# Accumulating transfers for three blocks of a context job's softmax sums in a two-layer gated attention and expert kernel

## The chip, the core and the metric

The kernel runs on one core of a Trainium2 chip. The metric is the device time of one execution in microseconds (us), as the median of several runs. A profile of one execution is used to read where the time goes.

## The reference

Two layers are applied to x (2 x 1024 tokens of 512 features). Each adds an attention and then a mixture of eight experts, both gated by a tanh, to the residual. The first layer's attention is causal self-attention plus attention to a context (2 x 2048 tokens of 256 features); the second's is attention to the context alone. There are 16 heads of 32 features. What matters here is the attention:

```python
att = jnp.einsum('bhqd,bhkd->bhqk', q, k) * scale
...
y = jnp.einsum('bhqk,bhkd->bhqd', jax.nn.softmax(att, axis=-1), v)
...
attc = jnp.einsum('bhqd,bhkd->bhqk', qc, kc) * scale
y = y + jnp.einsum('bhqk,bhkd->bhqd', jax.nn.softmax(attc, axis=-1), vc)
```

All of it is in float32. A softmax needs, for every query, the sum of its exponentials over all keys; the changed part is how this sum is formed.

## The kernel before

The program is a row of phases: two projections, attention with self and context jobs ("attn0"), output and routing, experts, then a projection, attention with context jobs alone ("attn1"), output and routing, experts. Only the attention phases are touched.

An attention phase works on units: one batch entry and four heads (GH = 4) of one kind, causal or context. attn0 has eight units of each kind in turn, attn1 eight context units. A unit has four query blocks of 256 queries, and each is a *job*. A context job goes over all 2048 keys, 16 blocks of 128; a causal job over the blocks up to the diagonal, 2, 4, 6 or 8 of them. A job works in steps of two blocks (STEP = 2), so a context job has eight steps, called s0 to s7 below, and a block kb belongs to step kb // 2.

In a step, each engine has its part, in an order that the loops of the phase write out:

- TensorE ("PE") makes the scores of four items, each one block and two heads (`scores`, L714), works ahead on the maxima of later jobs (`maxima`, L686), and forms the products of the step before with the values (`values`, L731).
- ScalarE ("ACT") turns each item's scores into exponentials in `probs` (`exponent`, L803). `probs` is a ring of three steps, so an exponential of step m must wait until step m - 3 has been read by TensorE (`valued`) and by GpSimd (`added`). At a job's end ACT also copies the result out of PSUM (`drain`, L812).
- VectorE ("DVE") reduces the maxima (L844) and inverts the sums (`invert`, L861), in four pieces after the job's end.
- GpSimd ("POOL") adds the blocks named in `pooled` into `psums` (L662 for the first two, L665 for the others), and six steps after a job's end multiplies its result by the inverse (`normalize`, L642).
- SyncE ("SP") loads the keys, queries and values of later units and stores results.

The sum over the keys is shared out. TensorE could form it alone, by a matmul of a block's exponentials with ones (L738), four per block, one for each head. To spare it that, GpSimd adds ten blocks of a context job (0, 1, 2, 3, 4, 6, 7, 8, 10 and 12), and TensorE multiplies the sum `psums` by ones once, at the job's end (L746), after the values of the last step, when `added` says that the last add is done. The blocks 5, 9, 11, 13, 14 and 15 go through ones one by one. All these matmuls add up in half of one PSUM bank, and the value products in the other half.

`both`, `inv` and `y` are the buffers of a job's result on its way out: DEEP = 5 of each. The drain of a job must wait until the job that had the buffer before is normalised.

## Time and profile before

| what | value |
|---|---|
| median of 3 runs | 4098.98 us (4093.19 to 4100.37) |
| profiled execution | 4095.09 us |
| its span, first to last instruction | 4093.4 us |
| granted clock of TensorE, mean | 0.947 |
| TensorE, matmuls | busy 3706.0 us (91%) |
| VectorE | busy 2546.0 us (62%) |
| ScalarE | busy 2030.1 us (50%) |
| GpSimd | busy 1742.5 us (43%) |

The profile gives, for each instruction, its line, its start and its duration; idle time of an engine is put down to what ended it. Matmuls are pipelined, so their durations overlap, and time between the starts of two pieces says more than their busy time. A float32 matmul of this kernel appears as two records, so that a block of ones, four matmuls, is "x8". The timelines merge like instructions that follow each other into one row; the view by stretches gives the busy time of each engine between two times.

### The profile page before, as it was taken

The numbers are of one execution on the slowest core, as the hardware profiler recorded it, in microseconds if no ns is written. First come the engines' busy times: TensorE is split into PE (matmuls) and PEld (weight loads), VectorE is DVE, ScalarE is ACT, GpSimd is POOL, SyncE is SP. The second block draws the span as 40 slices with busy tenths as digits, with TensorE's granted clock in tenths as the row PEclk, the third lists the DMA queues.
The fourth block names the chain that finished last, engine by engine and source line by source line (L and its number), as shares of the span: only waits on it lengthen the run. The fifth ranks groups of instructions, "written<-read, shape, count | busy, mean of one in ns | idle before, by whom it ended". The sixth has DMA issues, their size and how long they took to land. (4 is left out here: it accounts for less than half of the span.)

```text
span 4093.4 us, 77661 instructions
## 1 busy us (share of the span) xinstructions
PE 3706.0 (91%) x30860; PEld 2602.1 (64%) x30860; DVE 2546.0 (62%) x3221; ACT 2030.1 (50%) x3561; POOL 1742.5 (43%) x854
## 2 busy tenths in 40 slices
PE   6989699999999997659996699999998659999997
PEld 5768456666666664459985355555554448888886
DVE  4345787878887883666664777777773664333442
ACT  2222266666666664136662366666664134434442
POOL 0000287778767775001110588888885001111110
PEclk9999799999999999779998799999998769999999
DMA  4478724433443433346653522323302233333341
GB/s 160 168 243 290 202 59 111 104 94 83 103 107 80 102 66 113 113 158 212 212 173 122 144 77 77 78 78 79 79 27 94 90 127 115 115 115 115 107 126 22
DMA packets 290273, 485.23 MB, mean 119 GB/s; under 512 B 23104, under 2 KB 121408, under 8 KB 287936
## 3 DMA queue, kind: packets, MB, share of 16 engines
q1 hardware_dynamic: 274368, 443.01, 36.2%
q0 software_dynamic: 14080, 37.76, 3.9%
q8 instruction: 208, 3.41, 0.4%
q14 instruction: 81, 0.66, 0.1%
q10 hardware_dynamic: 1536, 0.40, 0.0%
HBM read 350.67 MB, written 130.02 MB: 117 GB/s over the span
## 5 line engine op out<-in xcount | busy, mean ns | idle before, releaser
L803 ACT ACTIVATE attn_probs<-attn_low 128x512 f32<-128x512 f32 (+1 forms) x2368 | 1234.8, 595 | 465.9 <-PE attn_low L714 349.2
L844 DVE TENSOR_REDUCE attn_parts<-attn_mx 128x4 f32<-128x2048 f32 x538 | 1232.8, 2291 | 365.1 <-PE attn_mx L686 361.6
L665 POOL TENSOR_TENSOR attn_psums<-attn_psums,attn_probs 128x1024 f32<-128x1024 f32 x536 | 1275.0, 2379 | 67.6 <-ACT attn_probs L803 2.5
L714 PE MATMUL attn_low<-attn_queries,attn_keys 97*128 97x256 f32 (+1 forms) x4736 | 915.1, 311 | 11.7 <-DMA attn_queries<-attn_topT 5.6
L714 PEld LDWEIGHTS attn_low<-attn_queries,attn_keys 97*128 97x128 f32 x4736 | 658.4, 190 | 369.7 <-ACT attn_probs L803 188.0
L731 PE MATMUL attn_low<-attn_probs,attn_values 128*32 128x256 f32 x9472 | 629.4, 383 | 1.4 <-ACT attn_probs L803 1.4
L1488 DVE TENSOR_TENSOR ffn_wL<-ffn_raw,ffn_wH 128x2048 fp32r<-128x2048 f32 x128 | 293.4, 2292 | 223.1 <-ACT ffn_wH L1443 223.1
L1443 ACT ACTIVATE ffn_wH<-ffn_raw 128x2048 fp32r<-128x2048 f32 x128 | 245.3, 1916 | 338.2 <-DMA ffn_raw<-in_L_ffn_W_dram 177.4
L662 POOL TENSOR_TENSOR attn_psums<-attn_probs 128x1024 f32<-128x1024 f32 x88 | 209.8, 2384 | 369.3 <-ACT attn_probs L803 369.3
L731 PEld LDWEIGHTS attn_low<-attn_probs,attn_values 128*32 128x32 f32 x9472 | 247.6, 109 | 182.8 <-issue 2.0
L1400 PE MATMUL ffn_up<-ffn_xH,ffn_wH 128*128 128x256 f32 (+1 forms) x1024 | 348.2, 340 | 2.7 <-DVE ffn_xL L1494 2.7
L1400 PE MATMUL ffn_up<-ffn_xH,ffn_wL 128*128 128x256 f32 (+1 forms) x1024 | 349.0, 341 | 0.0
L1400 PE MATMUL ffn_up<-ffn_xL,ffn_wH 128*128 128x256 f32 (+1 forms) x1024 | 347.9, 340 | 0.0
L686 PE MATMUL attn_mx<-attn_keysn,attn_queriesn 32*128 32x512 f32 (+3 forms) x2388 | 298.8, 493 | 51.3 <-DMA attn_queriesn<-l_queries 26.5
L1415 PE MATMUL ffn_down<-ffn_wH,ffn_hH 128*128 128x512 f32 x768 | 306.7, 399 | 0.0
L1369 POOL DMA_INDIRECT out_dram<-ffn_yo,ffn_idx_out x32 | 53.8, 1680 | 592.9 <-DVE ffn_yo L1523 463.3
L1415 PE MATMUL ffn_down<-ffn_wH,ffn_hL 128*128 128x512 f32 x768 | 304.4, 396 | 0.0
L1415 PE MATMUL ffn_down<-ffn_wL,ffn_hH 128*128 128x512 f32 x768 | 304.3, 396 | 0.0
L738 PE MATMUL attn_low<-attn_probs,keep_onesf 128*32 128x256 f32 (+1 forms) x3776 | 266.5, 373 | 0.0
L1512 DVE TENSOR_TENSOR ffn_hL<-ffn_hf,ffn_hH 128x256 fp32r<-128x256 f32 (+1 forms) x256 | 138.3, 556 | 203.3 <-ACT ffn_hH L1464 203.3
L861 DVE RECIPROCAL attn_inv<-attn_both 128x64 f32<-128x64 f32 x384 | 201.0, 536 | 70.9 <-ACT attn_both L812 70.9
L1464 ACT ACTIVATE ffn_hf<-ffn_up,ffn_b1T 128x256 f32<-128x256 f32 (+1 forms) x256 | 149.4, 584 | 160.3 <-PE ffn_up L1400 160.1
(196 smaller groups left out, 4426.5 us busy)
## 6 DMA issues: line engine op xcount, KB each, us to landing
ffn_raw<-in_L_ffn_W_dram SPq DMA_DIRECT2D x128, 1024.0 KB, 5.4
attn_keys<-l_cross_keys SPq DMA_DIRECT2D x96, 512.0 KB, 6.9
attn_queries<-l_queries SPq DMA_DIRECT2D x48, 512.0 KB, 4.8
l_cross_keys<-projc_high SPq DMA_DIRECT2D x64, 256.0 KB, 2.2
l_cross_keys<-projc_lowp SPq DMA_DIRECT2D x64, 256.0 KB, 2.5
l_cross_values<-projc_vout SPq DMA_DIRECT2D x64, 256.0 KB, 2.6
attn_keysn<-l_cross_keys SPq DMA_DIRECT2D x16, 1024.0 KB, 5.0
attn_values<-l_cross_values SPq DMA_DIRECT2D x32, 512.0 KB, 7.9
```

The costliest lines, as they stand in the source:

```text
L662: pool.tensor_tensor(ps, probs[:, m % RING, 0, :, :], at, ALU.add).then_inc(added, 1)
L665: pool.tensor_tensor(ps, ps, at, ALU.add).then_inc(added, 1)
L686: mm = pe.matmul(room[:, h, at:at + cols], QN[b][rows_h, q0:q0 + P], KN[b][rows_h, part * BLK:part * BLK + cols], start=True, stop=True)
L714: mm = pe.matmul(out[:, n0:], KS[b][0:3 * HD + 1, h, kb * P:(kb + 1) * P], QS[b][0:3 * HD + 1, h, job.qb * QB + n0:(job.qb + 1) * QB], sta ...
L731: mm = pe.matmul(acc[h * HD:(h + 1) * HD, 0, n0:], VS[b][:, kb, h * HD:(h + 1) * HD], probs[:, m % RING, i, h, n0:], start=kb == 0, stop=k ...
L738: mm = pe.matmul(acc[h * HD:(h + 1) * HD, 1, n0:], c["onesf"][:, 0:HD], probs[:, m % RING, i, h, n0:], start=False, stop=False, skip_group ...
L803: act.activation(probs[:, m % RING, i // 2, heads, n0:], sc[:, item % SC, :].rearrange("p (h q) -> p h q", q=QB)[:, :, n0:], ACT.Exp, scal ...
L844: op = dve.tensor_reduce(into, seen, AX.X, ALU.max)
L1400: mm = pe.matmul(up[ft % UP][:, 0:k], w[:, cols], x[:, ch, :], start=n == 0, stop=n == 3 * C - 1)
L1415: mm = pe.matmul(down[st][:, :], h[:, ft, st * P:(st + 1) * P], w[:, cols], start=ft == 0 and n == 0, stop=ft == FT - 1 and n == 2)
L1443: act.activation(wH[:, m % RING, :], raw[:, m % RING, :], ACT.Copy).then_inc(high_made, 1)
L1488: dve.tensor_tensor(wL[:, m % RING, :], raw[:, m % RING, :], wH[:, m % RING, :].bitcast(F32), ALU.subtract).then_inc(low_made, 1)
```

## The change

In a context job, blocks 5, 9 and 11 are no longer summed by TensorE but added to block 1 by transfers that accumulate into SBUF. The exponentials of block 1 go not into the ring but into a buffer of their own, `heap` (two of them, for jobs in turn), from which the value products of block 1 read too. GpSimd issues the three transfers, at steps s2, s4 and s5, each ahead of that step's adds. The first waits until the value products of s0 have read the heap, the second and the third until the transfer before has landed (`heap_in`). At the job's end TensorE multiplies the heap by ones, after a wait for all three. ACT, before it writes over a step of the ring, waits for the transfer that reads from it.

GpSimd's own list becomes 2, 3, 4, 6, 7, 8, 10, 12 and 13: nine blocks and eight adds, where there were ten and nine. Blocks 0, 14 and 15 go through ones on TensorE. Causal jobs have no heap and keep their lists. DEEP becomes 3.

```diff
--- before.py
+++ after.py
@@ -421,7 +421,8 @@
         if unit.causal:
             self.pooled = [kb for kb in whole if kb < 2 or kb % 2 == 0]
         else:
-            self.pooled = [kb for kb in whole[:-3] if kb < 4 or kb == 7 or kb % 2 == 0]
+            self.pooled = [2, 3, 4, 6, 7, 8, 10, 12, 13]
+        self.heaped = () if unit.causal else (1, 5, 9, 11)
 
     def adds(self, step=None):
 
@@ -517,6 +518,19 @@
         done = sum(x.adds() for x in self.jobs if x.last < m)
         return done + sum(x.adds(m - x.first) for x in self.jobs if x.first < m <= x.last)
 
+    def heaps(self, j):
+
+        return sum(max(0, len(x.heaped) - 1) for x in self.jobs[j % 2:j:2])
+
+    def heaped_at(self, m):
+
+        if not 0 <= m < self.steps:
+            return 0, 0
+        job = self.jobs[self.job_of[m]]
+        s = m - job.first
+        return (len([kb for kb in job.heaped[1:] if kb // STEP == s]),
+                len([kb for kb in job.heaped[1:] if kb // STEP <= s]))
+
     def ends(self, m):
 
         j = self.job_of[m]
@@ -531,7 +545,7 @@
     plan = Plan(units)
     jobs, N_STEPS, N_JOBS = plan.jobs, plan.steps, len(plan.jobs)
     KEYS = max(u.keys for u in units)
-    RING, SC, DEEP = 3, 3, 5
+    RING, SC, DEEP = 3, 3, 3
     ROWS = GH * QB // P
     with Phase(nc, name) as ph:
         KS = [ph.sb(f"keys{b}", [P, GH, KEYS], F32R) for b in range(BUFS)]
@@ -548,6 +562,7 @@
         inv = [ph.sb(f"inv{d}", [P, QB]) for d in range(DEEP)]
         y = [ph.sb(f"y{d}", [P, QB]) for d in range(DEEP)]
         fence = ph.sb("fence", [P, BLK])
+        heap = [ph.sb(f"heap{d}", [P, GH, QB]) for d in range(2)]
         low = ph.ps("low", (P, SC + 1, BLK))
         mx = ph.ps("mx", (P, GH, BLK))
         sc, acc = low[:, 0:SC, :], low[:, SC, :].rearrange("p (a q) -> p a q", q=QB)
@@ -565,9 +580,17 @@
         stack_in = [ph.sem(f"stack_in{b}") for b in range(BUFS)]
         row_set = [ph.sem(f"row_set{d}") for d in range(ROWS_DEEP)]
         fence_set = ph.sem("fence_set")
+        heap_in = [c["keep"].sem(f"{name}_heap_in{d}") for d in range(2)]
         inverted = [ph.sem(f"inverted{d}") for d in range(DEEP)]
         y_out = [ph.sem(f"y_out{d}") for d in range(DEEP)]
         FLAT, STACK, ROW, PIECES = 2, 11, QB // P, 4
+
+        def block_of(m, i):
+
+            j = plan.job_of[m]
+            if jobs[j].heaped and (m - jobs[j].first) * STEP + i == jobs[j].heaped[0]:
+                return heap[j % 2]
+            return probs[:, m % RING, i, :, :]
 
         def load_flat(sp, u, piece):
             unit, b = units[u], u % BUFS
@@ -651,6 +674,16 @@
                     here = [kb for kb in job.pooled if kb // STEP == s]
                     k = plan.adds(m)
                     ps = psums[:, j % 2, :, :]
+                    for n, kb in enumerate(job.heaped[1:]):
+                        if kb // STEP != s:
+                            continue
+                        pool.wait_ge(exped, plan.item[m, 2 * (kb % STEP) + 1] + 1)
+                        if n:
+                            pool.wait_ge(heap_in[j % 2], DMA * (plan.heaps(j) + n))
+                        else:
+                            pool.wait_ge(valued, job.first + job.heaped[0] // STEP + 1)
+                        pool.dma_start(heap[j % 2][:, :, :], probs[:, m % RING, kb % STEP, :, :], accum_op=ALU.add
+                                       ).then_inc(heap_in[j % 2], DMA)
                     for kb in here:
                         at = probs[:, m % RING, kb % STEP, :, :]
                         if kb == job.pooled[0]:
@@ -729,10 +762,10 @@
                     for i, (kb, n0, _) in enumerate(here):
                         for h in range(GH):
                             mm = pe.matmul(acc[h * HD:(h + 1) * HD, 0, n0:], VS[b][:, kb, h * HD:(h + 1) * HD],
-                                           probs[:, m % RING, i, h, n0:], start=kb == 0,
+                                           block_of(m, i)[:, h, n0:], start=kb == 0,
                                            stop=kb == len(job.blocks) - 1, skip_group_check=True)
                     for i, (kb, n0, _) in enumerate(here):
-                        if kb in job.pooled:
+                        if kb in job.pooled or kb in job.heaped:
                             continue
                         for h in range(GH):
                             mm = pe.matmul(acc[h * HD:(h + 1) * HD, 1, n0:], c["onesf"][:, 0:HD],
@@ -741,6 +774,11 @@
                     mm.then_inc(valued, 1)
                     if m == job.last:
                         if job.pooled:
+                            if job.heaped:
+                                pe.wait_ge(heap_in[j % 2], DMA * (plan.heaps(j) + len(job.heaped) - 1))
+                                for h in range(GH):
+                                    pe.matmul(acc[h * HD:(h + 1) * HD, 1, :], c["onesf"][:, 0:HD], heap[j % 2][:, h, :],
+                                              start=False, stop=False, skip_group_check=True)
                             pe.wait_ge(added, plan.adds(m + 1))
                             for h in range(GH):
                                 mm = pe.matmul(acc[h * HD:(h + 1) * HD, 1, :], c["onesf"][:, 0:HD],
@@ -798,9 +836,15 @@
                         act.wait_ge(valued, m - RING + 1)
                         if plan.adds(m - RING + 1):
                             act.wait_ge(added, plan.adds(m - RING + 1))
+                        new, all_of = plan.heaped_at(m - RING)
+                        if new:
+                            before = plan.job_of[m - RING]
+                            act.wait_ge(heap_in[before % 2], DMA * (plan.heaps(before) + all_of))
                     act.wait_ge(scored, item + 1)
                     heads = slice(2 * (i % 2), 2 * (i % 2) + 2)
-                    act.activation(probs[:, m % RING, i // 2, heads, n0:],
+                    if job.heaped and m == job.first and i == 2 * job.heaped[0] and plan.job_of[m] >= 2:
+                        act.wait_ge(job_done, plan.job_of[m] - 1)
+                    act.activation(block_of(m, i // 2)[:, heads, n0:],
                                    sc[:, item % SC, :].rearrange("p (h q) -> p h q", q=QB)[:, :, n0:],
                                    ACT.Exp, scale=SCALE).then_inc(exped, 1)
```

The order of the instructions shows it on GpSimd, in the second attention stage, for one context job and the first add of the next. `psums` is GpSimd's sum, `y` the result that is normalised. Before:

```order
L662 TENSOR_TENSOR attn_psums<-attn_probs 128x1024
L665 TENSOR_TENSOR attn_psums<-attn_psums,attn_probs 128x1024 x6
L642 TENSOR_TENSOR attn_y<-attn_both,attn_inv 128x256
L665 TENSOR_TENSOR attn_psums<-attn_psums,attn_probs 128x1024 x2
L662 TENSOR_TENSOR attn_psums<-attn_probs 128x1024
```

And with the change (its lines are numbered anew):

```order
L695 TENSOR_TENSOR attn_psums<-attn_probs 128x1024
L685 DMA attn_heap<-attn_probs 128x1024
L698 TENSOR_TENSOR attn_psums<-attn_psums,attn_probs 128x1024 x3
L685 DMA attn_heap<-attn_probs 128x1024
L698 TENSOR_TENSOR attn_psums<-attn_psums,attn_probs 128x1024
L665 TENSOR_TENSOR attn_y<-attn_both,attn_inv 128x256
L685 DMA attn_heap<-attn_probs 128x1024
L698 TENSOR_TENSOR attn_psums<-attn_psums,attn_probs 128x1024 x3
L695 TENSOR_TENSOR attn_psums<-attn_probs 128x1024
```

One of the six adds ahead of the normalisation, and with it the two behind, are now parted by three transfers; there are eight adds in place of nine, and three of them, not two, stand behind the normalisation.

On TensorE, from the end of one context job (s7) through s0 of the next. `low` is the PSUM tile, in one part of which scores stand and in another the results; `onesf` are the ones. Before:

```order
L738 MATMUL attn_low<-attn_probs,keep_onesf 32x256 x8
L746 MATMUL attn_low<-attn_psums,keep_onesf 32x256 x4
L714 MATMUL attn_low<-attn_queries,attn_keys 128x256 x6
L686 MATMUL attn_mx<-attn_keysn,attn_queriesn 128x512 x4
L714 MATMUL attn_low<-attn_queries,attn_keys 128x256 x2
L731 MATMUL attn_low<-attn_probs,attn_values 32x256 x8
L714 MATMUL attn_low<-attn_queries,attn_keys 128x256 x6
```

And with the change:

```order
L771 MATMUL attn_low<-attn_probs,keep_onesf 32x256 x8
L780 MATMUL attn_low<-attn_heap,keep_onesf 32x256 x4
L784 MATMUL attn_low<-attn_psums,keep_onesf 32x256 x4
L747 MATMUL attn_low<-attn_queries,attn_keys 128x256 x6
L719 MATMUL attn_mx<-attn_keysn,attn_queriesn 128x512 x4
L747 MATMUL attn_low<-attn_queries,attn_keys 128x256 x2
L764 MATMUL attn_low<-attn_probs,attn_values 32x256 x4
L764 MATMUL attn_low<-attn_heap,attn_values 32x256 x4
L771 MATMUL attn_low<-attn_probs,keep_onesf 32x256 x4
L747 MATMUL attn_low<-attn_queries,attn_keys 128x256 x6
```

The heap's matmuls stand ahead of those of psums, and s0 now has a block of ones, that of block 0.

## Rows read from the trace of the kernel before

**Rows 1.** Page of the kernel before: its span

```profile
span 4093.4 us, 77661 instructions
```

**Rows 2.** Stretch table: length, PE, PEld, DVE, ACT, POOL busy, PEclk, DMA, GB/s

```profile
2390.00:2440.00 50.00, 49.71 (x552) 29.70 (x556) 39.03 (x26) 34.24 (x68) 42.72 (x20) 1.00 0.25 60
```

**Rows 3.** Timeline of PE (start, us, operation, records), context jobs of both stages

```profile
541.97 0.61 PE L746 MATMUL attn_low<-attn_psums,keep_onesf 128*32 128x256 f32 x8
...
567.74 0.61 PE L746 MATMUL attn_low<-attn_psums,keep_onesf 128*32 128x256 f32 x8
...
2617.13 1.07 PE L731 MATMUL attn_low<-attn_probs,attn_values 128*32 128x256 f32 x16
...
2620.03 1.07 PE L731 MATMUL attn_low<-attn_probs,attn_values 128*32 128x256 f32 x16
...
2622.93 1.07 PE L731 MATMUL attn_low<-attn_probs,attn_values 128*32 128x256 f32 x16
...
2626.15 1.07 PE L731 MATMUL attn_low<-attn_probs,attn_values 128*32 128x256 f32 x16
...
2639.73 1.05 PE L738 MATMUL attn_low<-attn_probs,keep_onesf 128*32 128x256 f32 x16
2640.59 0.61 PE L746 MATMUL attn_low<-attn_psums,keep_onesf 128*32 128x256 f32 x8
...
2642.90 1.07 PE L731 MATMUL attn_low<-attn_probs,attn_values 128*32 128x256 f32 x16
```

**Rows 4.** Timeline of POOL, the same job

```profile
2616.66 2.38 POOL L662 TENSOR_TENSOR attn_psums<-attn_probs 128x1024 f32<-128x1024 f32 x1 [2.73 <-ACT attn_probs L803]
2619.18 14.99 POOL L665 TENSOR_TENSOR attn_psums<-attn_psums,attn_probs 128x1024 f32<-128x1024 f32 x6
2634.14 0.73 POOL L642 TENSOR_TENSOR attn_y<-attn_both,attn_inv 128x256 f32<-128x256 f32 x1
2634.83 4.91 POOL L665 TENSOR_TENSOR attn_psums<-attn_psums,attn_probs 128x1024 f32<-128x1024 f32 x2
```

**Rows 5.** Timeline of ACT, the same job

```profile
2621.58 2.06 ACT L803 ACTIVATE attn_probs<-attn_low 128x512 f32<-128x512 f32 x4 [0.83 <-PE attn_low L714]
...
2635.67 1.57 ACT L803 ACTIVATE attn_probs<-attn_low 128x512 f32<-128x512 f32 x3 [0.82 <-ACT attn_probs L803]
```

**Rows 6.** Instructions of L665 (the adds): who waited for them, us, times

```profile
  PE attn_low L746: 1.8, 2
```

**Rows 7.** Transfers that POOL issues: issue times, landing times, GB/s in 40 slices

```profile
L234 POOL DMA_DIRECT2D projc_xin<-in_ctx_dram x7 | 5.2, 749 | 138.5 <-DVEq L348 138.5
...
1776.00 1.00 POOL L1358 DMA_INDIRECT ffn_xg<-xn,ffn_idx  x1 [0.30 <-issue]
...
L1369 POOL DMA_INDIRECT out_dram<-ffn_yo,ffn_idx_out x32: 1549/1618/2078, 3426.7 to 4082.2; - x32
...
projc_xin<-in_ctx_dram POOLq DMA_DIRECT2D x8, 512.0 KB, 5.1
...
GB/s 0 0 0 0 0 23 0 47 79 167 82 0 0 0 0 20 79 164 123 0 0 0 0 20 61 155 138 0 0 0 0 29 76 164 105 0 0 0 0 0
...
out_dram<-ffn_yo,ffn_idx_out POOLq DMA_INDIRECT x4, 4.7
```

**Rows 8.** Stretch table and timeline of PE after a wait, columns as in rows 2 and 3

```profile
113.80:117.20 3.40, 3.40 (x11) 2.74 (x10) 1.39 (x2) 0.62 (x2) 0.00 (x0) 0.57 0.17 60
...
112.53 1.57 PE L244 MATMUL proj_turn<-keep_ident,proj_xn 128*128 128x128 f32 x8 [3.24 <-DVE proj_xL L345]
...
115.18 0.63 PE L264 MATMUL proj_bank<-proj_xH,proj_wH 128*128 128x512 f32 x1
115.61 0.63 PE L264 MATMUL proj_bank<-proj_xL,proj_wH 128*128 128x512 f32 x1
...
117.29 0.39 PE L264 MATMUL proj_bank<-proj_xH,proj_wH 128*128 128x512 f32 x1
117.52 0.39 PE L264 MATMUL proj_bank<-proj_xL,proj_wH 128*128 128x512 f32 x1
```

## The prediction

> **What bounds the kernel now.** I read the page first for the span: 4093.4 us, in a profiled execution of 4095.09 us [rows 1]. The median of the three runs shown is 4098.98 us, 3.9 us above that execution; the sum below is made against 4095.1 and then lifted by 4 us.
>
> The change touches only context jobs of the two attention stages: 8 units x 4 query blocks in each, so **64 jobs** of 8 steps (s0 to s7). The stretch table is next: in 50 us of the second attention stage TensorE is busy 49.71 us at granted clock 1.00 and GpSimd 42.72 us, with the DMA engines at a quarter [rows 2]. So TensorE sets the pace and GpSimd has some 15% to spare; the reader should ask where in a job that spare time lies.
>
> TensorE's timeline answers for one job [rows 3]. The value products (L731) of s0 begin at 2617.13 and those of the next job's s0 at 2642.90: a period of **25.77 us**. The first stage has the same period: its matmuls on psums (L746) start at 541.97 and 567.74, 25.77 apart. A step without a matmul against the ones, s1, lasts 2622.93 - 2620.03 = 2.90; s2, with one such block (four matmuls, which the trace shows as 8 records), lasts 2626.15 - 2622.93 = 3.22. One block of ones is therefore worth **0.32 us** inside a job. In s7 blocks follow each other: two start at 2639.73 and the psums at 2640.59, so **0.43 us** each there.
>
> GpSimd's timeline of the same job [rows 4]: first add at 2616.66, six at 2619.18, the normalisation of the job before at 2634.14 (0.73 us), two more adds that end at 2634.83 + 4.91 = 2639.74. That is 23.08 us, or (23.08 - 0.73) / 9 = **2.48 us per add**, without a hole. TensorE reads the psums at 2640.59, 0.85 us later, and only 2 times was seen waiting for an add there, 1.8 us in all [rows 6]. GpSimd's slack thus lies before its first add, where it waits 2.7 us for the first exponentials of the new job; against the end of the job it has 0.85 us.
>
> **The change, part by part.** I measure from the time of the first add of before (2616.66 = 0). There, the psums are read at 23.93.
>
> TensorE: blocks 5, 9, 11 and 13 lose their ones matmuls in s2, s4, s5 and s6 (4 x 0.32 = 1.28 saved); block 0 gets one in s0 (0.32 more); the heap adds one block in s7 (0.43 more). The saving is 1.28 - 0.32 - 0.43 = **0.53 us per job**; all of it falls ahead of the psums, which TensorE would want at 23.93 - 0.53 = **23.4**, with a period of 25.24. Value matmuls keep their number.
>
> GpSimd: one add of nine goes. But the first add is now of blocks 2 and 3, a step later, and the order is: add, transfer of 5, three adds, transfer of 9, add, normalisation, transfer of 11, three adds. Transfer 5 stands ahead of the add of block 4 and waits for the last exponential of s2. ACT's group at 2621.58 holds four exponentials in 2.06 us, the first of them that one [rows 5]: 2621.58 + 0.52 - 2616.66 = 5.4, and 0.3 later for the ones of block 0, so 5.8. The first add, after s1's exponentials, is over by then. From there GpSimd has 7 adds (17.4), the normalisation (0.7), three issues of d each, and a stall s: 5.8 + 17.4 + 0.7 = 23.9 + 3d + s. TensorE, which wants the psums at 23.4, is late by **L = 0.5 + 3d + s**.
>
> The stall: transfer 11 may only go when 9 has landed, X after its issue began. Between the two GpSimd has its issue d, one add (2.5) and the normalisation (0.7), so s = X - d - 3.2. Queued behind it are the adds of 10, 12 and 13, and behind those TensorE's psums, the drain on ACT and the next job. Transfer 5 has three adds (7.5 us) to land in, which covers it.
>
> **d**, GpSimd's time for one issue. Before has no accumulating direct transfer. From below: a plain direct one of 512 KB took 0.75 us of GpSimd [rows 7], with the 0.1 that lies between its adds (2.48 for an add of 2.38 us) 0.85. From above: an accumulating indirect one took 1.55 to 1.62, and an issue behind a gather began 0.30 after it, so 1.85. A gather took 1.00, so adding costs up to 0.55; I take half of that on the 0.75, and 0.15 for the gap: **d = 1.2**.
>
> **X**, from issue to landing. From below: a plain transfer of 512 KB from GpSimd landed in 5.1. From above: 256 KB accumulated into DRAM landed in 4.7 [rows 7], so twice that, 9.4. Their stretch shows that these moved at 164 to 167 GB/s at best, so another 256 KB needs 1.6 us more: 4.7 + 1.6, less 0.3 for the shorter issue: **X = 6.0**. (The Trainium skill, "DMA: Bandwidth & Descriptors", Anatomy of one DMA, puts a transfer by GpSimd at about 2.0 us plus bytes / 436e3, which would be an estimate of 3.2 us here and would leave no stall: L = 0.5 + 3.6 = 4.1, 4328 us. The row of half the bytes at 4.7 us speaks against that figure.)
>
> **The sum.** s = 6.0 - 1.2 - 3.2 = 1.6. L = 0.5 + 3.6 + 1.6 = 5.7. Per job 5.7 - 0.53 = +5.2 us; 64 jobs give +331; 4095.1 + 331 + 4 = **4430 us**. GpSimd becomes the bound of the context jobs.
>
> What I cost at nothing, and its cover. ACT's first exponential of s7 now waits for transfer 9. It is issued at 5.8 + 1.2 + 7.4 = 14.4 and lands at 20.4; ACT wants it at 2635.67 - 2616.66 - 0.64 = 18.4, so TensorE loses 2 us in s7, but it then waits for the psums until 29.1 anyway. Transfer 11 is issued at 20.4, lands at 26.4, and holds ACT's first three exponentials of the next job until 28.0, again before 29.1. If GpSimd were on time, these two would be late next. Three result buffers instead of five: the drain of a job waits for the normalisation three jobs back, in a context job long done; in the short causal jobs there is one step (2.9 us) to spare; were that lost, one step in each of 8 units is 23 us. The traffic of the transfers lies on DMA engines that are three quarters idle.
>
> **Rivals.**
> 1. *The issue is free*: GpSimd's adds run on while descriptors are written, d = 0. Then s = 2.8, L = 3.3, +2.8 per job, **4276 us**. Against it: a gather that follows another begins 0.30 after its 1.00 us, not at once [rows 7].
> 2. *Nothing changes*: d = 0, and the transfers land within 3.2 us. L = 0.5 eats the saving: **4099 us**. No landing in the rows is that short for so many bytes.
> 3. *Faster*: GpSimd isn't late at the psums, and TensorE's 0.53 us count in full: 64 x 0.53 = 34, **4065 us**. It decides at a chain under 23.4: d = 0, no stall, and adds without the 0.1 between them (7 x 0.1 = 0.7). Before shows that gap in every run of adds.
> 4. *Slow transfers*: X = 9.4, so s = 5.0, L = 9.1, **4647 us**, from which point transfer 11 is what TensorE waits for. For it: packets of loads share the engines.
> 5. *The clock falls*: TensorE stands some 4 us per job. After one wait of 3.24 us the granted clock was 0.57 in the next 3.4 us, that is mostly 1.2 instead of 2.4 GHz, and matmuls there started 0.43 instead of 0.23 apart [rows 8]: some 1.4 us lost. At one such loss per job: +90, **4520 us**. Against it: the heap's matmuls and those on the next scores break the wait up. (The Trainium skill, "TensorE: Matmul & The Clock Gate", The HAM clock gate, has the clock fall back to half rate when the engine idles; by that rule each job would lose it, and the wait in the row agrees.)
> 6. That the change doesn't do what it says can be left out: the order of instructions shows the matmuls leave and the transfers enter as described.
>
> **How the numbers follow.** The forecast's own case has 67%, the free issue 10%, the clock 9%, slow transfers 8%, nothing 3%, faster 3%. At d = 0.85 and X = 5.1 the sum gives s = 1.05, L = 4.1, 4328; at d = 1.85 with X = 6.0, 4514; at X = 9.4, 4647. The range goes from 4270, to take in the free issue, to 4650, which leaves out about one part in eight. Only "nothing" and "faster" are not slower by over 0.2%, which is about what a measurement of this kernel can tell from no change: faster 3%, same 3%, slower 94%.
>
> **What would show it.** Right: the period between matmuls on psums near 31 us in both attention stages; TensorE waiting for GpSimd's adds once per context job for several us; GpSimd's last three adds ending just ahead of the psums; a stall on GpSimd in front of the third transfer; issue rows of 0.85 to 1.85 us; other stages unchanged. Wrong: a period at or under 25.8; GpSimd with time to spare ahead of the psums; the wait for the heap in place of that for the adds; the third transfer issued without a stall.

## The result, and the profile after

The change made the kernel slower: **4560.19 us** median of 4 runs (4554.03 to 4565.9) against 4098.0 us of the kernel before on the same chip (4093.19 to 4100.37), a ratio of 1.1129 with a 95% interval of 1.1116 to 1.1143. That is +462 us; forecast were 4430, within 4270 to 4650.

The page of the changed kernel (span; GpSimd's adds; the transfers' issue, and their median landing), which answers to [rows 1]:

```profile
span 4564.3 us, 76167 instructions
...
L698 POOL TENSOR_TENSOR attn_psums<-attn_psums,attn_probs 128x1024 f32<-128x1024 f32 x472 | 1176.7, 2493 | 39.0
...
L685 POOL DMA_DIRECT2D attn_heap<-attn_probs x192 | 166.4, 867 | 201.7 <-DMA attn_heap<-attn_probs 122.0
...
attn_heap<-attn_probs POOLq DMA_DIRECT2D x192, 512.0 KB, 4.9
```

The stretch table over the two attention stages, of the kernel before and then of the changed one (columns as in [rows 2]: length, PE, PEld, DVE, ACT, POOL busy, PEclk, DMA, GB/s):

```profile
470.00:1600.00 1130.00, 1108.92 (x12429) 685.72 (x12429) 881.40 (x1058) 745.06 (x1470) 841.94 (x400) 0.99 0.36 88
2285.00:3135.00 850.00, 825.56 (x8964) 492.83 (x8964) 636.18 (x411) 561.92 (x1089) 706.12 (x320) 0.98 0.27 70
```

```profile
470.00:1825.00 1355.00, 1215.30 (x11917) 720.77 (x11917) 881.34 (x1058) 748.27 (x1470) 849.39 (x464) 0.89 0.50 111
2515.00:3605.00 1090.00, 940.92 (x8448) 531.96 (x8448) 634.84 (x410) 567.28 (x1089) 712.74 (x384) 0.85 0.46 101
```

The whole loss lies here: 2445 us in place of 1980, +465. TensorE was busy 222 us longer although it does fewer matmuls, and stood still 289 us in place of 46, +243. So about half is waiting and half is matmuls that take longer: the granted clock fell from 0.99 and 0.98 to 0.89 and 0.85.

Who waits (engine, line, who ended the wait: us, times, longest):

```profile
ACT attn_probs L847 <- DMA attn_heap<-attn_probs: 376.6, 115, 8.6
...
POOL attn_heap L685 <- DMA attn_heap<-attn_probs: 122.0, 61, 5.1
...
PE attn_low L780 <- DMA attn_heap<-attn_probs: 74.8, 34, 5.6
PE attn_low L784 <- POOL attn_psums L698: 73.0, 45, 3.1
...
PE attn_low L747 <- ACT attn_probs L847: 54.2, 63, 4.3
...
PE attn_low L730 <- ACT attn_probs L847: 18.7, 5, 3.9
```

TensorE now waits for two things at a job's end: for GpSimd's adds, as forecast (2 waits in [rows 6]), and, in jobs that the forecast had not set apart, for the heap.

It waits as long, 54.2 + 18.7 = 73 us, in the middle of jobs, for exponentials of ACT, mostly where ACT could not write them yet because a transfer still read from the ring. Before, its waits for ACT at the scores were short:

```profile
PE attn_low L714 <- ACT attn_probs L803: 5.2, 25, 0.3
```

One such wait, on ACT and behind it on TensorE:

```profile
2891.93 2.08 ACT L847 ACTIVATE attn_probs<-attn_low 128x512 f32<-128x512 f32 x4 [5.52 <-DMA attn_heap<-attn_probs]
...
2892.58 1.77 PE L747 MATMUL attn_low<-attn_queries,attn_keys 97*128 97x256 f32 x6 [4.31 <-ACT attn_probs L847]
```

GpSimd's timeline, in two jobs that follow each other (start, us, then the idle time before):

```profile
2613.08 0.86 POOL L685 DMA_DIRECT2D attn_heap<-attn_probs  x1 [1.55 <-ACT attn_probs L847]
...
2620.03 0.86 POOL L685 DMA_DIRECT2D attn_heap<-attn_probs  x1 [2.99 <-DMA attn_heap<-attn_probs]
...
2637.84 0.88 POOL L685 DMA_DIRECT2D attn_heap<-attn_probs  x1 [0.62 <-ACT attn_probs L847]
2638.42 7.75 POOL L698 TENSOR_TENSOR attn_psums<-attn_psums,attn_probs 128x1024 f32<-128x1024 f32 x3
2646.12 0.85 POOL L685 DMA_DIRECT2D attn_heap<-attn_probs  x1
2646.68 2.69 POOL L698 TENSOR_TENSOR attn_psums<-attn_psums,attn_probs 128x1024 f32<-128x1024 f32 x1
2649.02 1.04 POOL L665 TENSOR_TENSOR attn_y<-attn_both,attn_inv 128x256 f32<-128x256 f32 x1
2651.41 0.87 POOL L685 DMA_DIRECT2D attn_heap<-attn_probs  x1 [1.35 <-DMA attn_heap<-attn_probs]
2651.99 7.67 POOL L698 TENSOR_TENSOR attn_psums<-attn_psums,attn_probs 128x1024 f32<-128x1024 f32 x3
```

In the second job the chain is as forecast: an issue, three adds, an issue, an add, the normalisation, a stall of 1.35 us, an issue, three adds. In the first, the third transfer had to wait 2.99 us, since the second took 6.95 us and not 5.29. The same two stretches in the stretch table:

```profile
2613.08:2620.03 6.95, 6.90 (x75) 4.14 (x75) 5.54 (x3) 4.46 (x10) 3.96 (x3) 1.00 1.03 267
2646.12:2651.41 5.29, 4.87 (x51) 2.66 (x51) 4.07 (x2) 2.92 (x7) 3.94 (x5) 1.00 0.61 126
```

In the slow one the DMA engines were full (1.03, 267 GB/s): loads for a later unit went at the same time. By the packets of the trace, the second transfer took over 5.5 us in 17 of 63 jobs. In ten of these, where it took 7.4 us or more, TensorE stood for 3.6 to 4.3 us in mid-job.

TensorE's timeline at the end of a job that loses its clock, and of the job shown above:

```profile
2590.05 0.64 PE L780 MATMUL attn_low<-attn_heap,keep_onesf 128*32 128x256 f32 x8 [3.16 <-DMA attn_heap<-attn_probs]
...
2599.69 1.94 PE L764 MATMUL attn_low<-attn_probs,attn_values 128*32 128x256 f32 x16
...
2604.59 1.94 PE L764 MATMUL attn_low<-attn_probs,attn_values 128*32 128x256 f32 x16
...
2629.88 0.60 PE L784 MATMUL attn_low<-attn_psums,keep_onesf 128*32 128x256 f32 x8
...
2656.10 0.64 PE L780 MATMUL attn_low<-attn_heap,keep_onesf 128*32 128x256 f32 x8 [0.19 <-DMA attn_heap<-attn_probs]
2659.72 0.74 PE L784 MATMUL attn_low<-attn_psums,keep_onesf 128*32 128x256 f32 x8 [2.98 <-POOL attn_psums L698]
2660.39 1.65 PE L747 MATMUL attn_low<-attn_queries,attn_keys 97*128 97x256 f32 x6
```

After the wait of 3.16 us the value products of a step take 1.94 us, not 1.07 [rows 3], and a step 2604.59 - 2599.69 = 4.90 us, not 2.90: the lower of the two clocks, 1.2 instead of 2.4 GHz, for most of that job (granted clock 0.66 from 2597 to 2630). From 2629.88 to 2659.72 the clock was full and the period is 29.84 us; there TensorE waits 2.98 us for the adds.

**The account by jobs.** I took the 63 intervals between matmuls on psums that are one context job each, from TensorE's timeline, and in each the time at less than the full granted clock. Before, they average 25.87 us, none with a low clock. After, 18 undisturbed ones (under 1 us at low clock) average 29.88; the other 45 average 34.2, with 521 us at low clock in all. Undisturbed lengthening: 64 x (29.88 - 25.87) = 257 us. What is left, 462 - 257 = 205 us, is nearly all in the jobs that lose clock: 45 x (34.2 - 29.88) = 194 us. By TensorE's longest wait around each fall of the clock in the context jobs, 23 of 68 falls go with a wait for the adds, 18 with one for the heap, 20 with one in mid-job for ACT, and 7 with one for the row of maxima (see the run list).

### The profile page after: what moved, and what is told of

The parts are those of the page before. It is cut to its first block and busy times, and to the rows that moved or that the text cites. A ratio compares the mean times of both kernels' runs of the same rounds, so it can differ in the third digit from the quotient of the medians.

```text
span 4564.3 us, 76167 instructions
## 1 busy us (share of the span) xinstructions
PE 3931.5 (86%) x29836; PEld 2678.4 (59%) x29836; DVE 2546.0 (56%) x3221; ACT 2038.1 (45%) x3561; POOL 1756.0 (38%) x982
## 5 line engine op out<-in xcount | busy, mean ns | idle before, releaser
L847 ACT ACTIVATE attn_probs<-attn_low 128x512 f32<-128x512 f32 x2240 | 1179.2, 594 | 888.6 <-PE attn_low L747 405.9
L698 POOL TENSOR_TENSOR attn_psums<-attn_psums,attn_probs 128x1024 f32<-128x1024 f32 x472 | 1176.7, 2493 | 39.0
L747 PE MATMUL attn_low<-attn_queries,attn_keys 97*128 97x256 f32 (+1 forms) x4736 | 1018.0, 334 | 79.8 <-ACT attn_probs L847 54.2
L747 PEld LDWEIGHTS attn_low<-attn_queries,attn_keys 97*128 97x128 f32 x4736 | 732.1, 209 | 500.6 <-ACT attn_probs L847 242.9
L764 PE MATMUL attn_low<-attn_probs,attn_values 128*32 128x256 f32 (+1 forms) x8960 | 663.3, 415 | 1.7 <-ACT attn_probs L847 1.7
L719 PE MATMUL attn_mx<-attn_keysn,attn_queriesn 32*128 32x512 f32 (+3 forms) x2388 | 322.0, 532 | 57.4 <-DMA attn_queriesn<-l_queries 25.3
L685 POOL DMA_DIRECT2D attn_heap<-attn_probs x192 | 166.4, 867 | 201.7 <-DMA attn_heap<-attn_probs 122.0
```

Source lines behind the costliest of these rows:

```text
L698: pool.tensor_tensor(ps, ps, at, ALU.add).then_inc(added, 1)
L719: mm = pe.matmul(room[:, h, at:at + cols], QN[b][rows_h, q0:q0 + P], KN[b][rows_h, part * BLK:part * BLK + cols], start=True, stop=True)
L747: mm = pe.matmul(out[:, n0:], KS[b][0:3 * HD + 1, h, kb * P:(kb + 1) * P], QS[b][0:3 * HD + 1, h, job.qb * QB + n0:(job.qb + 1) * QB], sta ...
L764: mm = pe.matmul(acc[h * HD:(h + 1) * HD, 0, n0:], VS[b][:, kb, h * HD:(h + 1) * HD], block_of(m, i)[:, h, n0:], start=kb == 0, stop=kb == ...
L847: act.activation(block_of(m, i // 2)[:, heads, n0:], sc[:, item % SC, :].rearrange("p (h q) -> p h q", q=QB)[:, :, n0:], ACT.Exp, scale=SC ...
```

## The experiments

"Undisturbed" and "low clock" are meant as in that account.

**deep3**: the kernel before, with three result buffers.

```diff
-    RING, SC, DEEP = 3, 3, 5
+    RING, SC, DEEP = 3, 3, 3
```

> The kernel before with three result buffers instead of five and nothing else. Theory (the transfers and GpSimd's late chain are the whole cost): no difference, 4098 us, at most 8 us either way. Rival (drains wait for result buffers in the short causal jobs): up to 23 us more, all of it in the first attention stage.

4094.24 us, ratio 0.9994 (0.9985 to 1.0004). The buffers cost nothing, as the forecast had it.

**list**: the changed kernel without heap and transfers; TensorE sums 1, 5, 9 and 11 itself.

```diff
-        self.heaped = () if unit.causal else (1, 5, 9, 11)
+        self.heaped = ()
```

> The changed kernel without its heap and transfers: GpSimd keeps the new list of nine blocks with a first add one step later, and TensorE sums blocks 0, 1, 5, 9, 11, 14 and 15. Theory (the transfers make GpSimd late, not the list): GpSimd's eight adds from 3.3 us on end at 24.1, TensorE, with one block of ones more than before, wants them at 24.25, so TensorE stays the bound: 64 x 0.32 = 20 us more than before, 4118 us (4105 to 4140), granted clock in attention 1.00. Rival (the late start of the adds alone makes GpSimd late): over 4200 us.

4187.66 us, 1.0213 (1.0186 to 1.024): more than expected, and under the rival's. TensorE hardly waits for the adds (4.0 us in all); what it waits for is this:

```profile
PE attn_low L747 <- DMA attn_queries<-attn_topT: 41.9, 35, 3.9
```

Before, TensorE waited 5.6 us, 4 times, for these small transfers, by which ACT puts the row of maxima beside the queries of the next job. The timeline of one job end, then of one of the kernel before (SPq and ACTq are transfers that SyncE and ACT issue):

```profile
2803.86 0.27 PE L730 MATMUL attn_low<-keep_ident,attn_top 128*8 128x128 f32 x1
...
2803.99 0.31 SPq L608 DMA_DIRECT2D attn_keys<-l_cross_keys  x1
...
2804.48 1.19 ACTq L828 DMA_DIRECT2D attn_queries<-attn_topT  x2
...
2808.72 0.74 PE L747 MATMUL attn_low<-attn_queries,attn_keys 97*128 97x256 f32 x4 [1.41 <-DMA attn_queries<-attn_topT]
```

```profile
2633.70 0.27 PE L697 MATMUL attn_low<-keep_ident,attn_top 128*8 128x128 f32 x1
...
2634.31 1.23 ACTq L790 DMA_DIRECT2D attn_queries<-attn_topT  x2
...
2635.28 0.46 SPq L585 DMA_DIRECT2D attn_keys<-l_cross_keys  x1
```

The row is turned (transposed, L730) at 2803.86, one step ahead of the scores that need it. Without block 13's ones in s6 that step is shorter by one block, but the row also lands later. Before, the load of a later unit's keys went out behind the row, 1.58 us after the turn; SyncE issues it behind the store of a result, which waits for GpSimd's normalisation. Here GpSimd normalises earlier (at 2802.08, 1.8 us ahead of the turn; in [rows 4] 0.4 us behind it), and the load goes out 0.13 us after the turn, ahead of the row. By the packets of the trace, rows with such a load ahead of them (42) landed 3.5 us after the turn in the median, and TensorE waited for 29; the others (47) landed after 2.55 us, and it waited for 2. That the load is the reason is read from the trace; no run moves the load alone. A third limit of a job's end, then, that neither theory had; early4 tests it.

**thin**: the transfers carry 32 of 1024 columns. Most of the sums of blocks 5, 9 and 11 is left out.

```diff
-pool.dma_start(heap[j % 2][:, :, :], probs[:, m % RING, kb % STEP, :, :], accum_op=ALU.add
+pool.dma_start(heap[j % 2][:, 0, 0:32], probs[:, m % RING, kb % STEP, 0, 0:32], accum_op=ALU.add
```

> The changed kernel with transfers that move 32 of 1024 columns, still 128 rows each, so most of the sums of blocks 5, 9 and 11 is left out. Issues and waits stay, the bytes go. Theory (issue time and the stall for the landing both count, and the long waits lower the clock): landing near 2.5 us, no stall in front of the third transfer, no waits of ACT or TensorE for the heap; what stays is L = 0.5 + 3 x 0.67 = 2.5 us, a period near 27.8, with waits too short for the clock: 4098 + 64 x 2.0 = 4226 us (4190 to 4300). Rival (the issues and the order alone cost what was measured, bytes and landing don't matter): over 4450 us.

4423.44 us, 1.0794 (1.0768 to 1.0819). The stall in front of the third transfer nearly went (GpSimd waits 17.7 us for landings, not 122.0), the chain did not:

```profile
DMA to landing us min/median/max: 2.0/2.6/6.3
```

```profile
PE attn_low L784 <- POOL attn_psums L698: 165.3, 61, 4.4
...
PE attn_low L780 <- DMA attn_heap<-attn_probs: 8.0, 13, 1.7
```

Undisturbed jobs last 28.66 us, 1.2 less than with the full transfers, about the stall of 1.35. But 47 jobs have time at low clock (314 us), now after waits for the adds almost alone (50 of 54 falls). Of the miss of 197 us, undisturbed jobs longer than expected are 64 x (28.66 - 27.8) = 55; the rest is in jobs that lose clock, which the expectation had ruled out. The bytes are worth only 137 us of the 462.

**fill**: where TensorE stands ahead of the heap it does 24 matmuls against zero weights (`nil`, set to zero in a part of the edit that is not shown). The sums are unchanged.

```diff
                             if job.heaped:
+                                for _ in range(6):
+                                    for h in range(GH):
+                                        pe.matmul(acc[h * HD:(h + 1) * HD, 1, :], nil[:, :], VS[b][:, 0:2, :],
+                                                  start=False, stop=False, skip_group_check=True)
                                 pe.wait_ge(heap_in[j % 2], DMA * (plan.heaps(j) + len(job.heaped) - 1))
```

> The changed kernel with 24 more matmuls (six blocks of four, weights zero, added to the sums as zeros) ahead of TensorE's wait for the heap at each context job's end: 2.6 us of work at the full clock in a wait of 3 to 6 us. Theory (the fall of the clock in these waits is nearly half of the loss): far fewer falls, periods nearer 29.7, 4350 us (4300 to 4450). Rival (the clock is low only while TensorE has nothing to do that matters): 4560 us or more.

4454.75 us, 1.0879 (1.086 to 1.0897): 105 us faster than the changed kernel with 24 matmuls a job more, and just over the expected range. Its stretch table:

```profile
470.00:1770.00 1300.00, 1214.16 (x13453) 731.11 (x13453) 881.68 (x1058) 742.90 (x1470) 850.77 (x464) 0.96 0.52 116
2470.00:3495.00 1025.00, 940.49 (x9971) 543.12 (x9971) 624.66 (x404) 559.77 (x1087) 713.91 (x384) 0.94 0.48 105
```

Undisturbed jobs keep their length (29.96), low clock goes from 521 to 167 us: 105 / 354 = 0.30 us won per us at low clock. At that rate the 521 us are worth 155 us; the account left 205 for the clock and the late landings together. What is left at low clock is no longer at the job's end: 28 of 32 falls go with a wait in mid-job for ACT, which no added matmul fills.

**two**: transfer 11 is left out, TensorE sums block 11.

```diff
-        self.heaped = () if unit.causal else (1, 5, 9, 11)
+        self.heaped = () if unit.causal else (1, 5, 9)
```

> The changed kernel without its third transfer: block 11 goes through ones on TensorE, blocks 5 and 9 are still added to the heap, GpSimd's list stays. Theory (GpSimd's late chain sets the end, the third transfer brings an issue of 0.6 us and a stall of 1.2 us to it): GpSimd reaches the end of its adds at 5.8 + 17.4 + 0.7 + 0.5 + 1.2 = 25.6 us, TensorE wants them at 23.7, period near 27.4, short waits, few falls of the clock: 4098 + 64 x 1.7 = 4207 us (4180 to 4260). Rival (the third transfer is only one of three alike, each a third of the loss): 4098 + 462 x 2/3 = 4406 us.

4301.68 us, 1.0494 (1.0477 to 1.0512). That lies between the two expectations. Without the third transfer TensorE never waits for the heap itself, and for the adds less; its largest wait is now the one for ACT:

```profile
ACT attn_probs L847 <- DMA attn_heap<-attn_probs: 137.0, 69, 5.5
...
PE attn_low L747 <- ACT attn_probs L847: 44.9, 52, 4.2
PE attn_low L784 <- POOL attn_psums L698: 43.3, 42, 1.6
```

Undisturbed jobs last 27.65 us, and 170 us are at low clock, with 21 of 34 falls at a wait for ACT and 11 at one for the adds, though none of these is over 1.6 us. More than half of the loss (259 us) hangs on the third transfer.

**short**: blocks 12 and 13 go from GpSimd to TensorE.

```diff
-            self.pooled = [2, 3, 4, 6, 7, 8, 10, 12, 13]
+            self.pooled = [2, 3, 4, 6, 7, 8, 10]
```

> The changed kernel with its three transfers, but GpSimd adds only seven blocks (2, 3, 4, 6, 7, 8, 10) and TensorE also sums 12 and 13. GpSimd's adds then end near 22.5 us, ahead of TensorE, which wants them near 24. Theory (once the adds are on time, the third landing is next): period between 26.0 (TensorE alone) and 28.5 (third transfer landing 7.6 us after its issue), 4112 to 4270 us, and no waiting of TensorE for GpSimd's adds. Rival (the transfers themselves, not the chain of adds, make up the loss): 4450 us or more.

4390.42 us, 1.0716 (1.0682 to 1.075), between the two. The adds are on time: no wait of TensorE for them is left. The heap is what it waits for, as before:

```profile
ACT attn_probs L847 <- DMA attn_heap<-attn_probs: 401.9, 125, 7.9
...
POOL attn_heap L685 <- DMA attn_heap<-attn_probs: 129.6, 62, 5.8
...
PE attn_low L780 <- DMA attn_heap<-attn_probs: 77.0, 32, 5.1
```

So the late adds were only one of two waits at the same place: with GpSimd's adds on time, transfer 11, held up by 9, is late next.

**early** and **early2**: GpSimd begins to add at block 0 again, in s0; the heap starts from block 3; transfers of 4 and 8 have their steps to land in. early has a third one, of 12, in s6; early2 gives 12 to TensorE. The rest of the edit, not shown, sets the steps in which GpSimd adds.

```diff
-            self.pooled = [2, 3, 4, 6, 7, 8, 10, 12, 13]
-        self.heaped = () if unit.causal else (1, 5, 9, 11)
+            self.pooled = [0, 1, 2, 5, 6, 7, 9, 10, 11]
+        self.heaped = () if unit.causal else (3, 4, 8, 12)
...
+        self.heaped = () if unit.causal else (3, 4, 8)
```

> The same three transfers and eight adds, placed anew: GpSimd adds 0, 1, 2, 5, 6, 7, 9, 10, 11, so its first add is at s0 again; the heap starts with block 3, transfers of 4, 8 and 12 at s2, s4 and s6; TensorE sums 13, 14 and 15. Theory (the late chain and the stall are the loss, the saving on TensorE is real): chain of 8 x 2.5 + 0.7 + 3 x 0.6 + 0.5 = 23.0 us against 23.4: 4064 us where the transfers land in 5 us, up to 1.5 us more per job where they land in 7.6: 4060 to 4200 us. Rival (accumulating transfers cost wherever they stand): over 4300 us.

> As the kernel placed anew, but with the transfers of 4 and 8 alone; TensorE sums 12, 13, 14 and 15. GpSimd's chain is 22.4 us, the last landing far from the end. TensorE saves 4 x 0.32 - 2 x 0.4 - 0.43 = 0.05 us per job: 4095 us (4080 to 4130). Rival (any accumulating transfer costs): over 4200 us.

early 4380.71 us, 1.0686 (1.0662 to 1.0709); early2 4115.44 us, 1.005 (1.0034 to 1.0067). So early took the time of its rival, and early2 shows that the rival's reason is wrong. The wait of early, then those that end with a transfer of early2's heap:

```profile
PE attn_low L782 <- DMA attn_heap<-attn_probs: 140.9, 55, 5.6
```

```profile
POOL attn_heap L691 <- DMA attn_heap<-attn_probs: 18.5, 13, 2.4
ACT attn_probs L848 <- DMA attn_heap<-attn_probs: 17.3, 24, 1.5
```

In early2 two accumulating transfers per job, chained one behind the other, cost next to nothing (18 us in all, 0.5%): 26.08 us a job, no low clock, and TensorE not once waiting for the heap. One more at the job's end costs 265 us (331 us of low clock). It seldom has to wait for the one before it (GpSimd waits 15.5 us for landings in early, 11 times, against 122.0, 61 times, in the changed kernel), so what makes it dear is that its own landing is wanted at once. A third transfer in an earlier place was not run.

**early3**: as early2, with 12 to GpSimd and 9 to TensorE.

```diff
-            self.pooled = [0, 1, 2, 5, 6, 7, 9, 10, 11]
+            self.pooled = [0, 1, 2, 5, 6, 7, 10, 11, 12]
```

> The chain of the run with two early transfers, with the sums dealt out anew: GpSimd adds blocks 0, 1, 2, 5, 6, 7, 10, 11, 12, the heap carries 3, 4, 8, TensorE sums 9, 13, 14, 15. In the traces so far a lone block of ones in a step lengthens it from 2.91 to 3.21 us, a second one beside it from 3.21 to 3.64. Steps of 2.33, 2.90, 2.91, 2.91, 2.91 (3.21 for s4), 2.91, 3.04, 3.27 and 2.19 to the psums, with the one lone block of s4 in it, come to about 25.7 us a job, against 25.87 in the kernel before; 64 jobs give -13 us: 4085 (4075 to 4098), clock as before. Rival: the two issues (0.57 us each) and the add of block 12 make GpSimd late again: TensorE waits for the adds in many jobs and the time is over 4115.

4154.92 us, 1.0145 (1.0127 to 1.0162): over 4115, as the rival had it, but not for its reason: TensorE waits for the adds 0.7 us in all. Again it is the row of maxima, and again behind a load (waits for 30 of 43 rows with one ahead, for 1 of 49 without):

```profile
PE attn_low L748 <- DMA attn_queries<-attn_topT: 37.1, 37, 4.2
```

**fill2**: more matmuls against zero weights, at four places (in the changed kernel).

```diff
+                    if job.heaped and m in (job.first, job.last - 1):
+                        fill(b, 3)
...
+                                fill(b, 6)
                                 pe.wait_ge(heap_in[j % 2], DMA * (plan.heaps(j) + len(job.heaped) - 1))
...
+                                fill(b, 3)
                             pe.wait_ge(added, plan.adds(m + 1))
```

> The changed kernel with more matmuls against zero weights where TensorE stands: 12 after the values of s0 and of s6, 24 ahead of the wait for the heap, 12 ahead of the wait for psums (results unchanged). If the clock's fall is what lies between the lengthened chain and the measured time, the time at low clock in context jobs goes under 60 us (521 in the changed kernel, 167 with 24 such matmuls) and undisturbed jobs keep 29.7 us; with the jobs whose second transfer is late that is 4350 to 4420 us. Rival: the excess is stalls of the late transfer and not the clock; then the time stays at 4455 or above although the low clock is gone.

4577.58 us, 1.1193 (1.1169 to 1.1217). The rival's numbers came, and still this does not decide for it: low clock is nearly gone (78 us), but undisturbed jobs last 32.0 us, 2.1 more, since part of the matmuls lay in no wait (from the value products of s0 to those of s1 4.51 us in the median, in fill 3.21). Filling pays only up to the wait's length.

**early4** and **turn**: the row of maxima of a context job is turned one step earlier, in early3 and in the kernel before.

```diff
-        turn = -1 if m < 0 else m + 2
+        turn = -1 if m < 0 else m + (2 if self.units[self.jobs[j].u].causal else 1)
```

> As the run before it with the sums dealt out anew (4154.92 us), and the row of maxima of the next context job is turned one step earlier. There, jobs without a wait for that row had a period of 25.47 us and the median job 26.5. Theory: the row's landing, which TensorE waited for in most jobs, is the whole rest; with one step (2.9 us) more the wait for it goes under 10 us in all and the period to 25.4 to 25.6: (25.87 - 25.5) x 64 = 24 us under the kernel before, 4074 (4060 to 4090). Rival: the turn then waits for VectorE's maxima, or GpSimd's adds and the heap hold ACT as before: over 4100.

> The kernel before with the row of maxima turned one step earlier in context jobs, and nothing else. It waited only 7 us for that row, so it gains nothing: 4090 to 4100, period 25.8. If it is faster by as much as the run beside it, that gain is the turn's and not the transfers'.

early4 4100.16 us, 1.0012 (1.0001 to 1.0023); turn 4090.3 us, 0.9988 (0.9978 to 0.9998). In early4 the wait for the row is gone, 4.5 us in place of 37.1, and with it 55 us (27 us at low clock became none):

```profile
PE attn_low L748 <- DMA attn_queries<-attn_topT: 4.5, 2, 4.2
```

That shows the third limit. The expected 4074 was missed by 26: the median job is 25.88 us, not 25.5; the step in which the row is now turned, beside block 9's ones, grew from 3.21 to 3.36. Both times lie about 0.1% from the kernel before, under the 0.2% that the forecast takes for no change. None of my kernels beats the one before by more than that. Against turn, which shares its earlier turn, early4 is 10 us slower: well placed, the transfers cost little, but they win nothing.

## Why the prediction was right, and where not

- **Direction and bound: right.** GpSimd's chain became what the context jobs wait for, with the stall before the third transfer, in both stages, and elsewhere nothing moved (span +471, the two stages +465). Not all of it is GpSimd's chain: TensorE waits as long for the heap, and as long again for ACT.
- **d = 1.2 us per issue: too large.** The row lasts 0.87, near the lower bound, but the next add starts 2638.42 - 2637.84 = 0.58 after the issue does. Three cost 1.7 us, not 3.6, and 0.58 is under the whole bracket of 0.85 to 1.85 (whose upper end also left out the longest of the accumulating rows, 2.08). Half the price of an accumulating indirect transfer was the wrong surcharge: that is a transfer of another kind.
- **Stall s = 1.6: near,** 1.35. X was 5.29 here, not 6.0, but the normalisation took 1.04 for 0.73. Seven adds took 7.70 + 2.34 + 7.67 = 17.7 for 17.4. (The Trainium skill, "DMA: Bandwidth & Descriptors", Anatomy of one DMA, gave 3.2 us as an estimate for X, and no stall; none of the 192 transfers landed in under 4.5, so the measurement decides against it.)
- **L = 5.7: measured 29.84 - 25.24 = 4.6.** The parts give 0.5 + 1.7 + 1.35 + 0.3 (adds) + 0.3 (normalisation) = 4.2; 0.3 more is that the first issue comes 7.96 us after the psums of the job before, not 7.64 as the forecast's times make it. With the chain as measured and a clock that holds, the time would have been 4098 + 257 = 4355.
- **The clock: the step that failed.** I gave it 9% and, as rival 5, 1.4 us a job, from the time at low clock after one wait [rows 8]. 45 of 63 jobs lost it, with 521 / 45 = 11.6 us at low clock each; at 0.30 to 0.35 us lost per us at low clock that is 155 to 180 us, 2.4 to 2.8 us a job. What I set against it, that the heap's matmuls and those on the next scores break the wait up, fell: the clock fell behind the 2.98 us wait although the heap's matmuls stood just ahead of it, and the scores from 2660.39 on took 1.65 us and not 0.98. (The Trainium skill, "TensorE: Matmul & The Clock Gate", The HAM clock gate, has the rate halved when the engine idles. The trace agrees: the granted clock is 0.66 from 2597 to 2630, behind the wait of 3.16 us.) That 4560 lies in the range, and near rival 5's 4520, is in part luck: a chain smaller than forecast (4355 for 4430) and 205 us that the sum had at nothing work against each other.
- **DMA traffic at nothing: wrong.** Engines three quarters idle on average were full in the stretch where units load. The landing of the second transfer, 4.2 us by its packets in most jobs, was up to 8.1 there, and TensorE then waits, first for ACT and then for the heap: rival 4, in a quarter of the jobs. The third took over 5.5 us in 32 of 64 jobs, up to 9.0; where the adds are late, their wait hides most of it.
- **ACT's hold at nothing: wrong where the second transfer is late.** ACT waits 377 us for the heap. In the undisturbed job 0.67 us of that reaches TensorE, ahead of 2651.69, and the wait for the adds hides it, as forecast. With a late second landing TensorE stands 3.6 to 4.3 us in mid-job; its waits for ACT there come to 73 us in all, and 20 of the 68 falls of the clock go with them. In short, where the cover is gone, ACT's hold and the heap are what is left.
- **Three result buffers at nothing: right** (deep3).

What stays open: how the 205 us split between the clock and the late landings. A straight line through the 63 jobs gives 0.35 us per us at low clock (about 180 us) and some 20 us for late second landings; fill gives 0.30. All 17 jobs with a late second landing also lose clock, so neither is separate.

## What to carry to other kernels

Price an accumulating transfer by where its landing is wanted: two of them with steps to land in cost 18 us here, one more at the job's end 265. Where a job already ends with 0.85 us of slack, list all that is wanted there (adds, heap, the next row of maxima), since curing one shows the next. Ask, too, which loads a new order on an engine lets out earlier, and what they then land ahead of. And count a wait that recurs on TensorE twice, once as waiting and once as the clock after it; here such waits, of some 3 us at a job's end and up to 4.3 us in mid-job, were followed by low clock in 45 of 63 jobs.

## What I had not expected of the hardware

- An accumulating transfer of 512 KB within SBUF takes 0.87 us as GpSimd's row but delays the next add by 0.58, and lands in 4.5 / 4.9 / 10.1 us (least, median, most). With 16 KB it lands in 2.0 / 2.6 / 6.3, so most of the longest time is not its bytes.
- Two rows of 2 KB, issued by ACT, were waited for 4.9 us after the turn that starts their way (2803.86 to 2808.72). By their packets they land in 2.55 us without a load ahead of them and in 3.5 (median) with one. A small transfer on a chain is priced by its latency, and by what was issued just before it.
- Idle TensorE can cost more than useless work: 24 matmuls against zeros in each job made the kernel 105 us faster.
